# A count loop over per-chunk windows of 128 targets, in steps of 64, in a four-layer graph kernel

## The reference, cut to what matters

```
h = relu(layernorm(x)); edge_index = [src, dst]
x = x + L0(h): m = relu(relu([h[src], h[dst]] @ Wm1 + bm1) @ Wm2 + bm2), summed by src; a matching term; two node layers
x = x + L1(h): three graph-attention layers with 4 heads over the edges
x = x + L2(h): the mean over each node's neighbours, then W and b
x = x + L3(h): sum over edges of edge_weight * h[src], by dst, then two layers
```

## Time and profile before

| | us |
|---|---|
| median of 3 runs (998.51 to 1005.07) | 999.43 |
| the profiled execution | 995.34 |
| its span, first to last instruction | 993.5 |
| PE busy | 876.5 (88%) |
| DVE busy | 666.2 (67%) |
| ACT busy | 502.4 (51%) |
| POOL busy | 291.9 (29%) |

### The profile page before, as it was taken

How to read it: one execution, slowest core, us unless ns; L and a number is a source line. 1 busy time by engine, 2 the same in 40 slices (tenths; PEclk the granted TensorE clock), 3 DMA queues, 4 the chain that set the end, 5 groups by cost and what they waited for, 6 DMA issues and landing times.

```text
span 993.5 us, 18362 instructions
## 1 busy us (share of the span) xinstructions
PE 876.5 (88%) x5355; PEld 545.8 (55%) x5356; DVE 666.2 (67%) x1778; ACT 502.4 (51%) x1006; POOL 291.9 (29%) x424
## 2 busy tenths in 40 slices
PE   3999958999899999999999998689978996899668
PEld 1556736878787878787878745322232222322134
DVE  6399985666666666666666763577757784967650
ACT  6232104555555556555555564466645674566521
POOL 5030036545444545454544400011132110121000
PEclk9999987999999999999999999799979998999979
DMA  3020032111111111111112300000000000000300
GB/s 80 28 81 1 1 115 66 42 63 51 60 49 59 48 63 47 59 50 56 53 55 47 68 1 1 1 0 1 1 1 0 1 1 0 1 1 0 132 38 21
DMA packets 19144, 35.85 MB, mean 36 GB/s; under 512 B 5280, under 2 KB 11552, under 8 KB 18976
## 3 DMA queue, kind: packets, MB, share of 16 engines
q0 software_dynamic: 7104, 19.41, 6.9%
q1 hardware_dynamic: 12000, 15.95, 4.8%
HBM read 29.56 MB, written 5.79 MB: 36 GB/s over the span
## 4 chain that ended last, share of the span: by engine, by line
PE 75%; DVE 13%; ACT 6%; issue 3%; DMA 1%; POOL 1%; DVEq 0%; ACTq 0%; POOLq 0%
PE PS L1374 9%; PE PS L1251 7%; PE PS L1245 6%; PE PS L1170 5%; PE PS L1359 5%; PE PS L1171 5%; PE PS L1185 5%; PE PS L1120 4%; PE PS L1365 4%; PE PS L1328 3%; PE PS L1242 3%; PE PS L1292 3%; DVE OHd L986 3%; PE PS L1163 3%; PE PS L1176 2%
## 5 line engine op out<-in xcount | busy, mean ns | idle before, releaser
L399 POOL DMA_INDIRECT BT<-Qtab,gidx x148 | 149.9, 1013 | 96.3 <-DVE gidx L813 61.2
L546 ACT ACTIVATE OHe<-OHs,sew 128x128 bf16<-128x128 bf16 x408 | 126.6, 390 | 63.5 <-PE PS L1251 63.0
L986 DVE CUSTOM_DVE_ANT_0 OHd<-PS,n1T 128x1024 bf16<-128x1024 f32 x96 | 112.1, 1220 | 19.5 <-PE PS L1328 19.5
L413 POOL TENSOR_SCALAR KV<-BT,pid 128x256 bf16<-128x256 uint8 x74 | 69.9, 945 | 176.2 <-DVE MS L888 170.8
L557 ACT ACTIVATE m2s<-m2s 128x512 f32<-128x512 f32 x68 | 42.8, 630 | 108.4 <-DVE m2s L914 108.4
L928 DVE TENSOR_SCALAR OHd<-iotaN,dstf 128x1024 bf16<-128x1024 f16 x136 | 64.0, 509 | 37.6 <-PE PS L1251 37.5
L1170 PE MATMUL PS<-Wm,m1T 128*128 128x256 f32 x276 | 83.2, 383 | 0.0
L914 DVE TENSOR_TENSOR m2s<-PS,bm 128x512 f32<-128x512 f32 x68 | 47.0, 691 | 53.6 <-PE PS L1171 53.6
L1171 PE MATMUL PS<-Wm,m1T 128*128 128x256 f32 x276 | 82.6, 381 | 0.0
L452 POOL TENSOR_TENSOR zl<-AL,Sx 128x8 f32<-128x8 f32 x12 | 2.6, 216 | 265.1 <-DVE Sx L986 265.1
L1251 PE MATMUL PS<-OHs,m2s 128*128 128x128 f32 x544 | 79.9, 291 | 0.0
(11 more groups left out here) (349 smaller groups left out, 1704.2 us busy)
## 6 DMA issues: line engine op xcount, KB each, us to landing
BT<-Wtab SPq DMA_DIRECT2D x1, 4096.0 KB, 12.8
BT<-Qtab,gidx POOLq DMA_INDIRECT x148, 2.8
BT<-Stab SPq DMA_DIRECT2D x1, 2048.0 KB, 10.2
Wtab<-H SPq DMA_DIRECT2D x4, 512.0 KB, 2.8
Wtab<-cs SPq DMA_DIRECT2D x4, 512.0 KB, 2.9
Qtab<-BT SPq DMA_DIRECT2D x1, 1024.0 KB, 4.5
Wn<-in_L_gnn_Wn SPq DMA_DIRECT2D x1, 1024.0 KB, 5.5
x<-in_x SPq DMA_DIRECT2D x1, 512.0 KB, 4.2
```

The lines of the kernel that those rows point to most:

```text
L399: g.indirect_dma_start(out=G[:, p % SLOTS, k, :], out_offset=None, in_=Qtab, in_offset=bass.IndirectOffsetOnAxis(ap=gidx[:, p, k:k + 1], a ...
L546: a.activation(OHe[:, k, j, :], OHs[:, k, :], ACT.Copy, scale=sew[:, j, bass.ds(2 * g + k, 1)])
L986: v.tensor_tensor_reduce(junk[n % 2], bank(4, 2), mask[:, i, :], 1.0, 2 * FAR, ALU.subtract, ALU.max, Sx[:, i, hd:hd + 1]).then_inc(S("gat ...
```

## The change: what it does

The range of targets is now found for each chunk and not for the pair. PE turns the columns `dstf` and `rngp` (now target times `valid`) into rows, DVE takes the least and the greatest over each chunk's 128 edges (`ends`), PE turns these back into rows on one partition, and DVE works out from them, in units of 64 targets, where each chunk's window of 128 targets begins and how many trips the pair takes. A window that starts in unit 7 or 15 would cross a PSUM bank, and a chunk that touches three or more units doesn't fit one window; if either chunk of a pair has one of these, both chunks of the pair start on an even unit. The trips of a pair are the greater of its two chunks'. `rngi` packs first unit of chunk 0, first unit of chunk 1, trips, and the source block. On PE one trip is now 2 chunks x (1 + 3) = 8 matmuls, each chunk at a place of its own, and the places are computed in registers in the loop. `inblk`, `flags`, `falling`, `nfrom` and the wait for `blocks_read` go. On DVE the two rounds over 32x576 (L845 to L857) and the fourteen small operations, 72 wide, behind the first message (L861 to L876) go; in their place fourteen mostly 144 wide ones on one partition stand ahead of the first message, and eight behind it.

```diff
+UNITS = 15 << 6
+WFIRST, WCOUNT, WBLK = 1 << 6, 1 << 10, 1 << 14
...
+        apart = sb("apart", [FEW, 2, NPAIR])
+        ends = sb("ends", [P, 2, 2])
...
+        unit_i = cs[:].rearrange("p b t -> p (b t)").bitcast(i32)[0:1, 0:4 * NCH].rearrange("p (u c) -> p u c", u=4)
+        unit = H[:].rearrange("p b t -> p (b t)")[0:1, 0:4 * NCH].rearrange("p (u c) -> p u c", u=4)
...
-            g.tensor_scalar(pblk[:, 1, 0:NPAIR - 2], pblk[:, 0, 2:NPAIR], float(NB * NB), None, ALU.mult)
+            g.tensor_scalar(pblk[:, 1, 0:NPAIR - 2], pblk[:, 0, 2:NPAIR], float(WBLK), None, ALU.mult)
...
-            v.tensor_copy(paired(dstf), sdst)
-            link(v.tensor_scalar(paired(skey), sdst, 7, None, ALU.arith_shift_right))
-            link(v.tensor_copy(sew0[:], skey[:]))
-            link(v.scalar_tensor_tensor(rngp[:], sew0[:], 1.0, valid[:], ALU.add, ALU.mult))
-            v.tensor_tensor(inblk, rngp[:].unsqueeze(1).to_broadcast([P, NB, NCH]),
-                            iota[:, 1:NB + 1].unsqueeze(2).to_broadcast([P, NB, NCH]), ALU.is_equal)\
-                .then_inc(S("blocks_marked"), 1)
+            v.tensor_copy(paired(dstf), sdst).then_inc(S("dst_ready"), 1)
+            eng.wait_ge(S("dst_ready"), 1)
+            v.scalar_tensor_tensor(rngp[:], dstf[:], 0.0, valid[:], ALU.add, ALU.mult).then_inc(S("dst_ready"), 1)
...
+            eng.wait_ge(S("dst_turned"), 1)
+            turned = bank(6).rearrange("p (m u e) -> p m u e", m=2, u=2)
+            v.tensor_reduce(ends[:, 0, :], turned[:, 0, :, :], AX.X, ALU.min).then_inc(S("ends_found"), 1)
+            v.tensor_reduce(ends[:, 1, :], turned[:, 1, :, :], AX.X, ALU.max).then_inc(S("ends_found"), 1)
...
-            eng.wait_ge(S("blocks_counted"), 1)
...
+            eng.wait_ge(S("ends_turned"), 1)
+            row = lambda m: unit_i[:, m, :]
+            link(v.tensor_copy(unit_i[:, 0:2, :], bank(7)[0:1, 0:2 * NCH].rearrange("p (m c) -> p m c", m=2)))
+            link(v.tensor_scalar(unit_i[:, 0:2, :], unit_i[:, 0:2, :], 6, None, ALU.arith_shift_right))
+            v.tensor_scalar(row(2), row(0), 7, None, ALU.bitwise_and)
+            link(v.tensor_scalar(row(3), row(0), 1, None, ALU.bitwise_and))
+            link(v.tensor_copy(unit, unit_i))
+            first, until, in8, odd = (unit[:, m, :].rearrange("p (g k) -> p g k", k=2) for m in range(4))
+            whole, count = apart[0:1, 0, :], apart[0:1, 1, :]
+            both = lambda t: t.unsqueeze(2).to_broadcast([1, NPAIR, 2])
+            spare = unit_i.bitcast(fp32)[:, 0, :].rearrange("p (g k) -> p g k", k=2)
+            link(v.tensor_tensor(until, until, first, ALU.max))
+            link(v.tensor_tensor(spare, until, first, ALU.subtract))
+            link(v.tensor_scalar(spare, spare, 2.0, None, ALU.is_ge))
+            link(v.scalar_tensor_tensor(in8, in8, 7.0, spare, ALU.is_equal, ALU.max))
+            link(v.tensor_tensor(whole, in8[:, :, 0], in8[:, :, 1], ALU.max))
+            link(v.tensor_tensor(odd, odd, both(whole), ALU.mult))
+            link(v.tensor_tensor(first, first, odd, ALU.subtract))
+            link(v.scalar_tensor_tensor(until, until, 2.0, first, ALU.add, ALU.subtract))
+            link(v.tensor_tensor(count, until[:, :, 0], until[:, :, 1], ALU.max))
...
             v.tensor_tensor(MS[:], made, G[:, 0, :, :], ALU.add).then_inc(S("msg_ready"), 1)
...
+            link(v.tensor_copy(rngi[0:1, :], count))
+            link(v.tensor_scalar(rngi[0:1, :], rngi[0:1, :], 1, None, ALU.arith_shift_right))
+            link(v.tensor_copy(count, rngi[0:1, :]))
+            link(v.tensor_scalar(whole, count, -2.0, float(2 * NB), ALU.mult, ALU.add))
+            link(v.tensor_tensor(first, first, both(whole), ALU.min))
+            link(v.scalar_tensor_tensor(whole, first[:, :, 0], float(WFIRST), first[:, :, 1], ALU.mult, ALU.add))
...
+            link(v.tensor_tensor(whole, whole, pblk[0:1, 1, :], ALU.add))
+            v.scalar_tensor_tensor(rngi[0:1, :], count, float(WCOUNT), whole, ALU.mult, ALU.add)\
                 .then_inc(S("spans"), 1)
...
-            eng.wait_ge(S("blocks_marked"), 1)
-            for u in range(2):
-                marks = inblk[:, u * NB // 2:(u + 1) * NB // 2, :].rearrange("p b (g k) -> p b g k", k=2)
-                for k in range(2):
-                    last = t.matmul(bank(6 + u)[0:FEW, 0:NB // 2 * NPAIR], onesb[:, 0:FEW], marks[:, :, :, k],
-                                    start=(k == 0), stop=(k == 1))
-            last.then_inc(S("blocks_counted"), 1)
+            eng.wait_ge(S("dst_ready"), 2)
+            t.matmul(bank(6), zeros[:, 0:P], zeros[:, 0:BANK], start=True, stop=True)
+            for m, column in enumerate((dstf, rngp)):
+                t.transpose(bank(6)[:, 2 * m * P:(2 * m + 1) * P], column[:, 0:P], ident[:])
+                last = t.transpose(bank(6)[0:NCH - P, (2 * m + 1) * P:(2 * m + 2) * P], column[:, P:NCH], ident[:])
+            last.then_inc(S("dst_turned"), 1)
+            eng.wait_ge(S("ends_found"), 2)
+            for m in range(2):
+                t.transpose(bank(7)[0:1, m * NCH:m * NCH + P], ends[:, m, 0:1], ident[:])
+                last = t.transpose(bank(7)[0:1, m * NCH + P:(m + 1) * NCH], ends[0:NCH - P, m, 1:2],
+                                   ident[0:NCH - P, 0:NCH - P])
+            last.then_inc(S("ends_turned"), 1)
...
                     eng.wait_ge(S("spans"), 1)
-                    span = eng.value_load(rngi[0:1, bass.ds(g, 1)], min_val=1, max_val=NB * NB * NB - 1)
+                    span = eng.value_load(rngi[0:1, bass.ds(g, 1)], min_val=1, max_val=NB * WBLK - 1)
...
-                    sources((g + 2) & (SLOTS - 1), (span >> 6) & (NB - 1))
+                    sources((g + 2) & (SLOTS - 1), (span >> 14) & (NB - 1))
...
-                    with eng.Fori((span >> 3) & 7, (span & 7) + 1, 2) as d:
-                        for k in range(2):
-                            for i in range(2):
-                                at = d * P + i * P
-                                dst = OHd[:, k, bass.ds(at, P)]
-                                t.matmul(PS[:, bass.ds(at, P)], OHc[:, k, :], dst,
+                    first, second = span & UNITS, span << 6
+                    with eng.Fori(first, first + ((span >> 3) & (2 * UNITS)), P) as d:
+                        for k, at in enumerate((eng.snap(d & UNITS), eng.snap((second - first + d) & UNITS))):
+                            dst = OHd[:, k, bass.ds(at, P)]
+                            t.matmul(PS[:, bass.ds(at, P)], OHc[:, k, :], dst,
+                                     start=False, stop=False, skip_group_check=True)
+                            for j in range(3):
+                                t.matmul(PS[:, bass.ds(at + 2 * BANK, P)], OHe[:, k, j, :], dst,
                                          start=False, stop=False, skip_group_check=True)
-                                for j in range(3):
-                                    t.matmul(PS[:, bass.ds(at + 2 * BANK, P)], OHe[:, k, j, :], dst,
-                                             start=False, stop=False, skip_group_check=True)
```

More of the change, by code:

```diff
@@ L150, in gnn_kernel @@
         FEW = 32
-        rngf = sb("rngf", [FEW, 2, NPAIR])
+        apart = sb("apart", [FEW, 2, NPAIR])
+        ends = sb("ends", [P, 2, 2])
         rngi = sb("rngi", [FEW, NPAIR], i32)
[L153 to L156, removed]
+        unit_i = cs[:].rearrange("p b t -> p (b t)").bitcast(i32)[0:1, 0:4 * NCH].rearrange("p (u c) -> p u c", u=4)
+        unit = H[:].rearrange("p b t -> p (b t)")[0:1, 0:4 * NCH].rearrange("p (u c) -> p u c", u=4)
         Wn1 = sb("Wn1", [P, 4, 4 * D])
@@ L748, in _ @@
             eng.wait_ge(S("iotas"), 3)
-            v.tensor_scalar(falling[:], iota[:, 0:NB], -1.0, float(NB), ALU.mult, ALU.add)
             v.tensor_scalar(before[:], iota[:, 0:P], pid[:], None, ALU.is_gt).then_inc(S("order_ready"), 1)
@@ L860, in _ @@
             v.tensor_tensor(MS[:], made, G[:, 0, :, :], ALU.add).then_inc(S("msg_ready"), 1)
[L861 to L866, removed]
-            link(v.tensor_copy(rngi[:], rngf[:, 1, :]))
-            link(v.tensor_scalar(rngi[:], rngi[:], 1, None, ALU.arith_shift_right))
-            link(v.tensor_copy(rngf[:, 1, :], rngi[:]))
-            link(v.tensor_scalar(nfrom[:], rngf[:, 1, :], -2.0, float(NB), ALU.mult, ALU.add))
-            link(v.tensor_tensor(nfrom[:], nfrom[:], rngf[:, 0, :], ALU.min))
-            link(v.tensor_scalar(rngf[:, 1, :], rngf[:, 1, :], 2.0, -1.0, ALU.mult, ALU.add))
-            link(v.tensor_tensor(rngf[:, 1, :], rngf[:, 1, :], nfrom[:], ALU.add))
+            link(v.tensor_copy(rngi[0:1, :], count))
[4 more added lines that the diff above has]
+            link(v.scalar_tensor_tensor(whole, first[:, :, 0], float(WFIRST), first[:, :, 1], ALU.mult, ALU.add))
             eng.wait_ge(S("pair_blocks"), 1)
-            link(v.tensor_tensor(rngf[:, 1, :], rngf[:, 1, :], pblk[:, 1, :], ALU.add))
```

(4 more changed lines are left out.)

## The result

| | us |
|---|---|
| before, on the same chip (median of 4) | 998.97 |
| after (1034.01 to 1039.3) | 1036.22 |
| ratio, 95% interval | 1.036 (1.031 to 1.041) |
| span profiled, before and after | 993.5, 1032.2 |

The change costs 37 us. The page says that PE now does less and the program takes longer: it shows 4896 matmuls where there were 5355, and PE's busy share falls from 88% to 86% (its modelled busy time, 876.5 us before, even grows with the span). PE's part of the chain that ended last shrinks while "issue" grows. The line of the chain is shown after and before.

The account below looks back on a forecast made before the run. PE's sequencer, working through register instructions on the pair's path, was taken as the bound. Terms +15.4, -1.5, +27.7, +2.2 and -0.7 gave +43 us: 1038 from the profiled 995.34 (1042 on the median), bounds 1027 to 1062, range 990 to 1064.

Parts of the forecast that it names:

- The bound: In the pair loop, PE's sequencer is on the path, each register instruction a step of 0.10 us; ordinary pair 5.48 us.
- the first rival: Count loop: matmuls set the pace and register work hides behind queued work; -28 us, 971; chance of faster 0.15.
- The trips: Count loop: trips rise from 71 to 84, 13 pairs go from one to two; matmuls fall from 1136 to 672.
- One trip, in register instructions: Count loop on PE: six more instructions at head and end, two fewer in the body; +0.32 us per one-trip pair.
- The second trip: Count loop, pairs with two trips: a second trip goes from 1.39 to 1.81 us, bounds 1.64 to 2.01.
- +27.7: Loop term in us for the 13 pairs going from one trip to two: 13 x (0.32 + 1.81).
- The third rival: Loop: granted clock may fall behind 16 two-trip pairs, some +14 us on top, 1056; chance 0.05.
- the predicted 13.9: Loop: us added by 52 pairs that stay at one trip, +15.4 for 48 and -1.5 for four at lower clock.
- Pairs at the lower clock: Four pairs after an idle PE, clock 0.50: the count goes from 1.82 to 1.44 us, -0.38 each.
- Ahead of the loop: Before the pair loop: DVE's changed operations and earlier second message, -0.7 us, bounds -1.5 and +2.
- the marks named beforehand: Signs in the loop afterwards: 672 matmuls, count 0.9 us, idle ahead 0.8, ordinary pairs 5.8, two-trip pairs about 7.6.
- the second rival: Count loop: window arithmetic done once ahead of the loop, places cheap; -5 us, 994, pairs stay at 5.5; chance 0.13.

Follow-up runs that it names:

- e1: The changed kernel with each count matmul issued twice from the same registers: 1037.09 us, 1.035 of the kernel before.
- e3: The kernel before with four more masks of the place d at the head of each trip: 1027.84 us, 1.026 of the kernel before.
- e14: The kernel before with only the load and check of the pair's word moved ahead of the wait for ranks_read: 958.72 us, 0.962 of the kernel before.
- e11: The changed kernel with the load of the pair's word moved ahead of the wait for ranks_read: 984.18 us, 0.989 of the kernel before.
- e9: The kernel before with word load, block and loop end worked out ahead of the ranks_read wait, kept in registers: 955.88 us, 0.960 of the kernel before.
- e8: The changed kernel with VectorE holding the trips in its words at one, so no second trips: 1001.16 us, 1.006 of the kernel before.
- e7: The changed kernel with one trip per pair fixed in the loop's bound, which the compiler folds: 992.65 us, 0.991 of the kernel before.
- e13: e9 with each count matmul issued twice from the same registers: 1016.18 us, 1.020 of the kernel before.

## Why the prediction was right, and where it wasn't

**The bound** was right: 672 more matmuls cost at most some 5 us (e1), five register instructions a trip 26 to 32 us (e3), and a load moved off the ring gave back 38 to 47 (e14, e11). PE's 88% busy said the opposite. The rule of the Trainium skill that spoke for the first rival (page "Advanced Engine Details and Errata", sections "Sequencer and Instruction Queues" and "Engine Queue Depths": engine instructions are pushed into a queue, 64 deep for TensorE, wait there, and others can be read and queued meanwhile) doesn't help here as long as the sequencer itself has to wait for DVE's ranks. In e9 it no longer does: the rank read that begins at 374.34 is over at 374.42, and the sequencer is at its own register work until after 374.8. There each matmul has its price.

**The trips** (71 to 84, 13 pairs more with two) were right.

**One trip, in register instructions** was the step that failed. "In the loop, ahead of its first matmul, there was one FUSED_REGOPS. Now there are seven" and "+0.32" for the pair. The lines of the pair at 422 to 424 us, head, chunks and end:

```profile
L1243 PEldq MOVE  x2: 29/33/37, 422.7 to 422.7; - x2
L1243 PEldq ALU_OP  x1: 32/32/32, 422.5 to 422.5; - x1
...
L1246 PEldq FUSED_REGOPS  x3: 60/74/124, 422.9 to 423.5; - x3
L1246 PEldq ALU_OP  x2: 32/32/32, 422.8 to 423.4; - x2
...
L1243 PEldq ALU_OP  x2: 32/38/43, 423.9 to 424.0; - x2
L1243 PEldq FUSED_REGOPS  x1: 73/73/73, 423.7 to 423.7; - x1
```

(Of the three fused ones of L1246, one stands ahead of the first matmul.) With the two fused ones of L1249 that is 13 steps ahead of the branch, where the kernel before has 12 and I had counted 16. A `snap` of an expression makes no MOVE. The second chunk's place is worked out between the matmuls of the first and the second, so the body is no shorter (0.71 from the first load to the end's first step, 0.70 before) and the head only one step longer. And the end's shift joins the step in one fused instruction. One step more is about 0.10; the median pair that stays at one trip is 0.13 longer. The 37 such periods that the clock left alone make 5 us, where all 48 pairs had been given 15.

**The second trip** was priced at 1.81, bounds 1.64 to 2.01; it measured 1.66, for the same reason. That is where the +27.7 became +23.3.

**The clock.** The third rival came about in part, as an addition to the forecast and at about half its price of 14 (16 pairs at its 0.7 would be 11). The sum had no term for it. Eight of the periods of pairs that stay at one trip are 0.6 to 1.2 longer, 8 us together. Four of these are those behind pairs with two trips early in the loop, four those behind a block's first pair. The stretch behind the sixth pair's two trips, columns as above:

```profile
197.40:201.00 3.60, 3.60 (x18) 3.36 (x19) 1.97 (x9) 2.17 (x7) 1.21 (x2) 0.53 0.24 73
```

Clock 0.53 (near its 1.2 GHz level) behind a pair whose array stood still for much of both trips; the kernel before has no such stretch there. That the array's pauses bring it on fits e1, where the pauses are shorter and the clock over the loop is 0.98 for 0.95, and e8, where three of these stretches go with the second trips. It isn't shown: behind the other twelve pairs with two trips there is no such stretch, and e8, with one trip a pair, keeps those behind the block starts. With the 5 above and -0.5 at six block starts this makes the 12.7 of the table: near the predicted 13.9, by another sum.

**Pairs at the lower clock** were right in kind and too small in size: the count of the sixth block's first pair takes 1.18 now, at a clock of 0.50 as before, where it took 1.82 and 1.44 was forecast. Matmuls do count there: with sixteen a trip at that clock, e1 needs 1.81 for the same count.

**Ahead of the loop** I had -0.7, and the loop line's first start is at 160.4, after 159.4. But this start is 158.9 in e1, whose instructions up to there are those of the changed kernel, and 158.9 and 160.6 in e8 and e7, which differ by one. So neither sign of the term is settled, nor is the +1.1 behind the loop, a stretch that varies by 2 us between the runs.

**Of the marks named beforehand**, the 672 matmuls held, and pairs of 5.6 and not 5.0 speak against the first rival. The others didn't: the idle time ahead of the count stayed at 0.36 and not 0.8, the count itself took 1.19 and not 0.9, the ordinary pair 5.6 and not 5.8, and two-trip pairs 7.2 to 7.3 and not 7.6. The ordinary pair is nearer the second rival's 5.5 than the forecast: the new places did come cheap, though not for the reason given there, and the loss is above all the second trips. The total came that near partly by luck: the steps were counted too high and the clock was left out, and these errors have opposite signs.

## What to carry to other kernels

When "issue" ends an engine's idle time, read its sequencer's rows before its busy share: register work, loads and branches behind the last wait are on the path, and the cheapest remedy is to move them ahead of that wait. Before cutting an engine's work, double it from the same registers; if the time hardly moves, that work isn't the bound, and a cut gains only what instructions go with it. And count register instructions in the lowered form of a line, not in its source: places are worked out where they are first used, a line of masks can bring a MOVE with it, and a folded bound can add a quarter to a half to what the edit itself is worth (e7, e8).

## What the runs showed of the hardware

- A matmul of 128 columns with its weight load costs 0.053 us where the array is the bound (e13 against e9). The Trainium skill, page "TensorE: Matmul & The Clock Gate", section "Back-to-back issue gap", gives 81 ns sustained for this width; the measurement here decides.
- Register instructions with records of about 30 ns on PE's sequencer cost 0.07 to 0.09 us each on the path (e3, five a trip: 26 us by the ratio, 32 by the traces); the 0.10 of the prediction is the distance of their starts. Fused ones take more, 0.14 a step in the body. Two ALU_OPs and a longer fused one cost 0.13 to 0.22 a loop end (e7 against e8).
- A load of a register word with its address and check takes about 0.75 us of PE's sequencer (the load's own record 0.30 of it; the first of its four instructions starts at 401.6, what follows them at 402.4); moved ahead of the wait it gave 0.5 a pair until the next bound.
